# Products that nobody reads in TensorE's gaps behind the convolution, and the router's head and search in another order

## What is computed

```python
x = x + _L0_xattn_ref(ctx, ctx, _layernorm(x), ssm_kernel, D, 8)      # long convolution
# router of the first layer, on 2048 tokens, 16 experts, k = 128
xf = _layernorm(x).reshape(bs, h)
logits = xf @ router_w + router_b
S = jax.nn.softmax(logits, axis=-1)
G, idx = jax.lax.top_k(S.T, k)
tokens = xf[idx]
out = jnp.einsum('ekh,hd->ekd', tokens, expert_w) + expert_b          # one weight for all experts
weighted = G[..., None] * out
y = zeros.at[idx.reshape(-1)].add(weighted.reshape(-1, h))
# then the retention, which needs x + y, normalized, and Wh @ Wh.T of each head
```

## Time and profile before

| | |
|---|---|
| Median of 3 runs | 1074.72 us |
| Lowest, highest | 1074.69, 1085.26 us |
| The profiled execution's own time | 1080.36 us |
| Its span, first to last instruction | 1077.9 us |
| Mean granted TensorE clock | 0.992 of full |
| TensorE busy | 1044.6 us, 97% of the span |

### The profile page before, as it was taken

The page is one execution under the profiler, slowest core; times in us unless marked ns, Lnnn a source line. Parts: engine busy times, 40 slices in busy tenths (PEclk is TensorE's granted clock), DMA queues, the critical chain, the costliest instruction groups (busy, mean ns, idle before and its releaser), DMA issues.

```text
span 1077.9 us, 13182 instructions
## 1 busy us (share of the span) xinstructions
PE 1044.6 (97%) x4865; PEld 845.8 (78%) x4865; DVE 580.2 (54%) x1039; ACT 446.5 (41%) x794; POOL 615.1 (57%) x458
## 2 busy tenths in 40 slices
PE   6999998899999999999999999999999999999998
PEld 4777776566789988877788888888888888888886
DVE  7998998848865645784522524325333253332224
ACT  4666444721576557554333323233232233222232
POOL 4888887110334652211377766677766677767662
PEclk9999999889999999999999999999999999999999
DMA  7612110000010020032222221632225332232211
GB/s 247 219 49 67 51 50 20 1 1 1 14 66 1 5 66 1 1 151 119 90 106 74 74 77 70 201 139 93 74 74 171 136 126 73 74 112 93 87 60 40
DMA packets 24543, 85.48 MB, mean 79 GB/s; under 512 B 3152, under 2 KB 4832, under 8 KB 23712
## 3 DMA queue, kind: packets, MB, share of 16 engines
q1 hardware_dynamic: 22432, 81.24, 22.0%
q10 hardware_dynamic: 2048, 3.41, 0.9%
HBM read 74.86 MB, written 9.78 MB: 79 GB/s over the span
## 4 chain that ended last, share of the span: by engine, by line
PE 64%; DVE 1%; POOL 1%; issue 1%; ACT 0%; POOLq 0%
PE banks L318 21%; PE banks L320 20%; PE banks L319 20%; PE banks L313 1%; PE banks L1460 1%; PE banks L1469 0%; POOL wgl L665 0%; DVE stat L1726 0%; POOL gul L691 0%; DVE xres L2115 0%; POOL xtr L648 0%; PE banks L1526 0%; DVE hf L2126 0%; DVE xres L1993 0%; DVE xf L2002 0%
## 5 line engine op out<-in xcount | busy, mean ns | idle before, releaser
L2126 DVE TENSOR_TENSOR hf<-banks,silu 128x512 f32<-128x512 f32 x132 | 91.3, 691 | 323.5 <-PE banks L320 322.3
L691 POOL TENSOR_TENSOR gul<-wst,guh 128x1280 fp32r<-128x1280 f32 x44 | 129.9, 2952 | 142.8 <-DVE guh L2009 135.8
L701 POOL TENSOR_TENSOR hl<-hf,hh 128x512 fp32r<-128x512 f32 x129 | 178.3, 1412 | 8.6 <-ACT hh L1079 8.6
L1079 ACT ACTIVATE hh<-hf 128x512 fp32r<-128x512 f32 x132 | 83.6, 633 | 190.3 <-DVE hf L2126 190.3
L1115 PE MATMUL banks<-kv,strip 128*128 128x288 f32 x640 | 160.3, 410 | 1.5 <-DVE strip L1658 1.5
L1077 ACT ACTIVATE silu<-banks 128x512 f32<-128x512 f32 x132 | 78.9, 598 | 167.1 <-PE banks L320 167.0
L1115 PEld LDWEIGHTS banks<-kv,strip 128*128 128x128 f32 x640 | 121.3, 192 | 33.9 <-DVE strip L1658 1.9
L318 PE MATMUL banks<-xf,guh 128*128 128x512 f32 x352 | 137.2, 390 | 0.9 <-POOL gul L691 0.9
L319 PE MATMUL banks<-xf,guh 128*128 128x512 f32 x352 | 136.9, 389 | 0.0
L320 PE MATMUL banks<-xf,gul 128*128 128x512 f32 x352 | 136.9, 389 | 0.0
L586 POOL TENSOR_TENSOR rstd<-vare,mhalf 128x2 f32<-128x2 f32 x32 | 25.9, 810 | 159.1 <-DVE vare L1739 159.0
(11 more groups left out here) (292 smaller groups left out, 2211.9 us busy)
## 6 DMA issues: line engine op xcount, KB each, us to landing
wst<-in_chunk_w SPq DMA_DIRECT2D x44, 960.0 KB, 4.7
strip<-toep SPq DMA_DIRECT2D x29, 256.0 KB, 3.1
xf_s<-xf SPq DMA_DIRECT2D x2, 2048.0 KB, 7.1
out<-xres SPq DMA_DIRECT2D x16, 256.0 KB, 2.1
xf<-xf_s SPq DMA_DIRECT2D x8, 512.0 KB, 5.7
mk<-hot_s SPq DMA_DIRECT2D x14, 256.0 KB
xres<-in_x ACTq DMA_DIRECT2D x4, 512.0 KB, 7.5
xres<-in_x SPq DMA_DIRECT2D x2, 1024.0 KB, 5.4
```

The costliest lines, as they stand in the source:

```text
L691: pool.tensor_tensor(gul[:, u, :], wst[:, u, 0:GU_W], f(guh[:, u, :]), ALU.subtract).then_inc(gul_ready, 1)
L701: pool.tensor_tensor(hl[:, u, s, :], hf[:, s, :], f(hh[:, u, s, :]), ALU.subtract)\
L1079: act.activation(hh[:, u, s, :], hf[:, s, :], ACT.Copy).then_inc(hh_ready, 1)
L2126: dve.tensor_tensor(hf[:, s, :], banks[:, 7, :], silu[:, s % 2, :], ALU.mult).then_inc(mul_done, 1)
```

## The change

A new function `keep_clock(n, bank)` issues n products of `minus` with 512 columns of `ewh` into a bank that nobody reads. TensorE calls it with 9 between `turn_x(1)` and `turn_x(2)`, with 5 behind `turn_x(3)`, and with 2, 5 and 2 between the turns of the pipeline's fourth and fifth pair. Because these products read `minus` and `ewh`, the waits for `pick_set` and `wB_ready` are moved from behind `leave_low(0)` to ahead of `turn_x(0)`.

In the router, two expert parts between `by_token(2)` and `by_token(3)` and one part behind the retention's matrix are taken out; two are put between the softmax's transposes and the search's first round; and `start` does 10 parts in place of 9 ahead of its first turn. VectorE's `grl` moves from ahead of the search to behind the gates, the gates' product goes to bank 2, since bank 5 is read later now, and TensorE waits for `grl` only before `turn_c(1)`, which writes bank 5.

```diff
-            for i in range(4):
-                turn_x(i)
+            def keep_clock(n, bank):
+
+                for _ in range(n):
+                    pe.matmul(banks[:, bank, :], minus[:, :], ewh[:, 0, :], start=True, stop=True)
+
+            pe.wait_ge(pick_set, 3)
+            pe.wait_ge(wB_ready, 2 + KB)
+            turn_x(0)
+            turn_x(1)
+            keep_clock(9, 0)
+            turn_x(2)
+            turn_x(3)
+            keep_clock(5, 0)
             after(pe, END_CONV)
             turn_o(4)
             turn_o(5)
             leave_low(0)
-            pe.wait_ge(pick_set, 3)
-            pe.wait_ge(wB_ready, 2 + KB)
             for n in range(1, TILES // 2):
...
                 if n > 1:
+                    if n == 4:
+                        keep_clock(5, 3)
                     turn_x(2 * n)
+                    if n in (3, 4):
+                        keep_clock(2, 3)
                     turn_x(2 * n + 1)
...
             by_token(2)
-            expert_parts(2)
             by_token(3)
...
             mm.then_inc(g_done, 1)
-            expert_parts(1)
 
             pe.wait_ge(t_vec, 6)
             for c in range(2):
                 mm = pe.transpose(banks[:, 0, c * P:(c + 1) * P], lg[:, c * P:(c + 1) * P], ident)
             mm.then_inc(t_pe, 1)
+            expert_parts(2)
             for i in range(STEPS):
...
             pe.wait_ge(t_vec, 11)
-            pe.wait_ge(grl_ready, 1)
...
-                mm = pe.matmul(banks[:, 5, c * 8:(c + 1) * 8], st_[:, c * P:(c + 1) * P], tile_sel,
+                mm = pe.matmul(banks[:, 2, c * 8:(c + 1) * 8], st_[:, c * P:(c + 1) * P], tile_sel,
...
                 pe.wait_ge(xn_ready, TILES + t + 1)
+                if t == 1:
+                    pe.wait_ge(grl_ready, 1)
...
-                    expert_parts((9, 4, 4, KB * TILES)[n] if n < 4 else 0)
+                    expert_parts((10, 4, 4, KB * TILES)[n] if n < 4 else 0)
...
-            dve.wait_ge(grh_ready, 1)
-            dve.tensor_tensor(grl[:, :, :].rearrange("p h e -> p (h e)"), banks[:, 5, :],
-                              f(grh[:, :, :]).rearrange("p h e -> p (h e)"), ALU.subtract).then_inc(grl_ready, 1)
             dve.memset(onesr[:, :], 1.0)
...
             assert n_vec[0] == T_GATED
+            dve.wait_ge(grh_ready, 1)
+            dve.tensor_tensor(grl[:, :, :].rearrange("p h e -> p (h e)"), banks[:, 5, :],
+                              f(grh[:, :, :]).rearrange("p h e -> p (h e)"), ALU.subtract).then_inc(grl_ready, 1)
             dve.wait_ge(t_pe, 3)
-            step(dve.tensor_copy(gate[:, :], banks[:, 5, 0:TILES]))
+            step(dve.tensor_copy(gate[:, :], banks[:, 2, 0:TILES]))
```

## The result

The changed kernel takes 1080.17 us (median of 22 runs, 1077.63 to 1083.04), the kernel before 1076.99 us beside it (22 runs, 1074.34 to 1085.26): ratio 1.0029 with a 95% interval of 1.0016 to 1.0041. It is slower by 3.2 us, twice what was forecast. The profiled execution took 1081.12 us, with a span of 1078.6 us. Between executions of one kernel the times differ by more than this; the number that goes with it is the mean granted clock of TensorE: of 35 runs of the kernel before in one series, the 16 with a clock of 0.995 or more took 1073.7 to 1076.7 us, and the 9 with 0.990 or less took 1079.4 to 1084.9.

The account below looks back on a forecast made before the run. TensorE, busy 97% of the span, bounds the kernel. Terms 5.2 - 1.2 - 2.8 - 1.9 + 0.7 = 0.0 us, or +3.1 without the falls; the middle, +1.5, gives 1076.2 us, range 1071.5 to 1082.0.

Parts of the forecast that it names:

- Part 1: Behind the convolution: TensorE waits for GpSimd's ebx, products queue behind, VectorE's first addition comes later: +5.2 us (+3.5 to +9.2).
- Part 2: Pipeline's fourth and fifth pair: products fill idle time, the clock's fall at 201 goes: -1.2 us, between -1.2 and 0.
- Part 3: Router's head: softmax begins 2.0 us earlier, copy of the scores follows sooner: -2.8 us, at least -2.0.
- Part 4: Search: two expert parts ahead of the first sum, so no clock fall at 231.7: -1.9 us, between -1.9 and 0.
- Part 5: Behind the search: `start` does 10 parts in place of 9, paid whole, +0.7 us; `grl` lies in a wait, free.
- The middle between two sums: Whole kernel: +1.5 us, taken between 0.0 against the profiled execution and +3.1 without its falls at 201 and 231.
- the second sum: Execution without the clock falls at 201 and 231, so 5.2 - 2.8 + 0.7 = +3.1 us.
- Rival (a): Behind the convolution: the low clock lasts, +9.2 in place of +5.2 us, end +7.1, 1081.8 us; chance 0.15.
- Rival (b): Behind the convolution: ebx is done in time, the wait does not hold TensorE: -5.8, 1068.9 us; chance 0.07.
- (c): Search's rounds: router's gain is paid back, parts 3 and 5 cancel: +2.1 or +5.2, 1078.4 us in the middle; chance 0.11.
- The rule weighed: Low clock behind the convolution: by the skill, products restore it sooner than turns; part 1 then +3.5 to +5.2 us.

Follow-up runs that it names:

- e11: Kernel before with the wait for wB_ready moved ahead of the first turn and all 23 products, router as before: ratio 1.0074 to the kernel before.
- e7: Changed kernel, moved wait kept, without the 9 and 5 products behind the convolution: ratio 0.9988 to the kernel before.
- e1: Changed kernel, but TensorE waits ahead of its first turn only for wB_high, and for wB_ready where it did before: ratio 0.9979 to the kernel before.
- e8: Changed kernel, TensorE's code untouched, GpSimd making ebx behind its work for the convolution's 15th head, not its last: ratio 0.9969 to the kernel before.
- e4: Kernel before with only the wait for wB_ready moved ahead of the first turn, no products: ratio 1.0053 to the kernel before.
- e12: e4 run once more, unchanged: ratio 1.0057 to the kernel before.
- e9: e5 plus 2, 2, 2 and 5 products in the search's first four rounds and 3 and 6 at the retention's start: ratio 0.9963 to the kernel before.
- e10: e5 plus 3 and 6 products at the retention's start, none in the search's rounds: ratio 0.9968 to the kernel before.
- e5: e1 with GpSimd's low parts of the context held until VectorE's softmax is done: ratio 0.9964 to the kernel before.

## Why the prediction was right, point by point

The range held, and so did the sign; the forecast of +1.5 us was half of the measured +3.2. The time itself, forecast at 1076.2, came out 4.0 us higher, and 2.3 of that is the start: the median of the three runs shown was 1074.72, that of the 22 runs beside the changed kernel 1076.99.

**Part 1** said that the moved wait eats the idle time and that VectorE's first addition comes 5.2 us late. The trace has 5.17, with the idle time (4.66 against 4.5) and one fall of 3.4 us, as worked out. That the fall would last 3.4 us and not longer was taken over from the trace before and not derived; with the 6.8 us of e11 the term would have been larger, so the agreement to 0.1 us is in part luck. The view names "issue" where I had said GpSimd. The split (hold, then queued products) was found by e7 as 1.7 and 3.5. That this is the whole loss is shown by e1 and e8, which lie 5.4 and 6.5 us lower. **Part 2** (-1.2) measured -1.3 in the profiled execution.

**Part 3** is the term that was mis-sized: -2.8, measured -2.2. The 2.1 us of the earlier logits came, but of the 0.8 us behind them only 0.07 were left, because the earlier softmax ran beside GpSimd's low parts. The step that failed is that I moved VectorE's work and did not ask what GpSimd does at its new place.

**Part 4** (-1.9) measured -2.07 over the first five rounds (from the copy of the scores to the fifth decision, 15.22 and 13.15 us); the 0.2 us more are the second round, whose wait of 0.68 us before I had left out. Then 0.84 us of it went in the fall at 244.3 (the sixth and seventh round took 2.61 and 2.69 us from decision to decision, in place of 2.23). TensorE was idle for 0.71, 0.68 and 1.18 us in the rounds ahead of it. I had said that the clock should not fall in the first rounds, and had only counted the idle time that the change fills, not what stays between the rounds.

**Part 5** (+0.7) measured +0.78, and `grl` lay in its cover, with the gates' copy 0.05 us behind it.

**The middle between two sums.** The sum against the profiled execution was 0.0 and came to +1.1 in it, by parts 3 and 4. Against an execution without the falls at 201 and 231 it was +3.1, close to what the medians show (+3.2); I took the mean of the two. The evidence for the second sum lay in the table: the profiled execution was 5.6 us above the median of the runs shown, and its falls were part of that. Even so that closeness is partly luck: with part 3 at its measured -2.2 the second sum is +3.7, and the means of the 22 runs differ by 2.4 us and not by 3.2.

**Rival (a)**, the lasting low clock, happens, but rarely behind the hold: of the five profiled executions with the hold (the changed kernel, e4, e7, e11, e12) it lasted 6.8 us in e11 and 3.4 us in the others. **Rival (b)** is out by the timeline, **(c)** too: the rounds kept 2.56 and 2.23 us, but for the two in the fall. **The rule weighed**: the low clock behind the convolution ended after 8 turns and six of the products in the changed kernel, and after 16 turns and one product before, in 3.4 us both times. In e7 it ended after 3.4 us (182.6 to 186.0) with nothing but turns. The products did not bring it back sooner than turns alone. The Trainium skill ("TensorE: Matmul & The Clock Gate", Part 4) says that transposes do not count as TensorE being busy the same way as products; by that they should have, and these traces do not agree. Whether turns count less in keeping the clock up is not separated here.

## What to carry to other kernels

An instruction without a reader still has operands, and the wait for them stands at the head of its engine's queue: wait for the producer of just what it reads (here `wB_high`), not for the counter that happens to cover it, and look up in the trace when that counter's last step ends. Filler products are worth placing only in idle time that is sure to be there; queued behind a wait they are plain delay, 3.5 us of 5.2 here. And when the clock falls in some executions only, compare the runs' mean clock and spread, each against the kernel before in the same series, and do not go by the idle stretches of one profile: with partial fills falls still showed elsewhere. With the retention's start filled as well (e9, e10) none of 12 runs had a clock under 0.998; the ratio to the kernel before did not go lower by it.

## What the runs showed of the hardware that was not expected

A VectorE instruction on two SBUF operands waited for GpSimd: 128 x 256 elements took 1.16 to 1.18 us beside GpSimd's subtraction of 2.51 us, ending 0.3 us behind it, in every profiled kernel with the earlier softmax and GpSimd's work in its old place, and 0.43 us with GpSimd held back (e5). The softmax's first step, which reads one operand from PSUM, took 0.42 us beside the same subtraction.

A fall lasted 3.4, 6.8 or 10.2 us, each with TensorE busy nearly all the way: 187.4 to 190.8 and 231.7 to 242.0 before, 182.9 to 189.7 in e11, 303.3 to 313.6 in e5. No other length stands between 176 and 370 in any of the 14 profiled executions. What decides between them stays open.

The same program has falls in some executions and not in others. The 12 runs of e5 have mean clocks from 0.995 to 1.000 and times from 1071.3 us (1.000) to 1077.4 us (0.995, the profiled one, with the fall at 303). TensorE's idle times ahead of that fall are 0.72 and 1.67 us; the profiled executions of the kernel before and of the changed one have the same two idle times there and no fall. The times of the kernel before differ by up to 11 us in one series, with mean clocks from 0.998 to 0.987.
